# A one-core decoder layer: first layer norm in groups of tiles, one product for the last 64 shared channels

## The reference

```
x = x + attention(layernorm(x))            # 16 heads of 128, causal, W_Q W_K W_V W_O
x = x + cross_attention(layernorm(x), ctx) # 32 heads of 16, ctx 375 rows per sequence
x = x + moe(layernorm(x))

layernorm: (x - mean) / sqrt(var + 1e-5)
moe: shared expert: silu(x @ shared_gate.T) * (x @ shared_up.T) @ shared_down.T   # 704 channels
     routed: top 2 of 8 experts of 352 channels, weights normalised to sum 1
```

## Time and profile before

| what | value |
|---|---|
| median of three runs | 963.21 us |
| the profiled execution | 963.22 us |
| its span, first to last instruction | 961.4 us |
| TensorE busy | 928.0 us, 97% of the span |
| VectorE busy | 544.2 us, 57% |
| ScalarE busy | 455.5 us, 47% |
| GpSimd busy | 178.3 us, 19% |

### The profile page before, as it was taken

The page is one execution under the profiler, slowest core; times in us unless marked ns, Lnnn a source line. Parts: engine busy times, 40 slices in busy tenths (PEclk is TensorE's granted clock), DMA queues, the critical chain, the costliest instruction groups (busy, mean ns, idle before and its releaser), DMA issues.

```text
span 961.4 us, 17906 instructions
## 1 busy us (share of the span) xinstructions
PE 928.0 (97%) x7250; PEld 807.5 (84%) x7250; DVE 544.2 (57%) x1192; ACT 455.5 (47%) x1113; POOL 178.3 (19%) x137
## 2 busy tenths in 40 slices
PE   4999999999999999999999999999999999999995
PEld 3999999999999999877777777777778888999994
DVE  6254444444444445485645546555457766888882
ACT  3342323232323233446666666566575234665651
POOL 1220202020202022411011011011000710223232
PEclk9999999999999999999999999999999999999998
DMA  5210442020202003212110010010032685998973
GB/s 190 67 45 22 166 164 66 24 66 22 66 23 67 22 22 110 65 47 88 55 34 23 13 34 23 13 33 13 1 125 80 231 247 185 335 301 280 303 198 44
DMA packets 31329, 94.12 MB, mean 98 GB/s; under 512 B 6176, under 2 KB 9488, under 8 KB 29328
## 3 DMA queue, kind: packets, MB, share of 16 engines
q1 hardware_dynamic: 26944, 83.80, 25.6%
q0 software_dynamic: 4304, 9.19, 4.7%
HBM read 74.33 MB, written 16.81 MB: 95 GB/s over the span
## 4 chain that ended last, share of the span: by engine, by line
PE 90%; DVE 5%; ACT 2%; issue 1%; DMA 1%; SPq 0%; POOL 0%; DVEq 0%
PE bank L512 25%; PE bank L513 24%; PE bank L514 24%; PE bank L709 3%; PE bank L726 3%; PE bank L559 3%; PE bank L584 3%; PE bank L676 1%; PE bank L571 1%; PE bank L822 1%; PE bank L736 1%; PE bank L600 1%; PE bank L830 1%; DMA wqk_f<-wqk 1%; DVE kT L1528 1%
## 5 line engine op out<-in xcount | busy, mean ns | idle before, releaser
L1130 ACT ACTIVATE ee<-bank 125x448 f32<-125x448 f32 x192 | 91.0, 547 | 22.0 <-PE bank L709 21.0
L512 PE MATMUL bank<-xT_hi,wqk_hi 128*128 128x448 f32 x256 | 95.9, 375 | 1.4 <-DVE xT_lo L1367 1.4
L514 PE MATMUL bank<-xT_lo,wqk_hi 128*128 128x448 f32 x256 | 93.8, 366 | 0.0
L513 PE MATMUL bank<-xT_hi,wqk_lo 128*128 128x448 f32 x256 | 93.6, 365 | 0.0
L512 PE MATMUL bank<-wkv_hi,ctx_hi 128*125 128x512 f32 x192 | 80.3, 418 | 2.6 <-DVE kn L1519 2.0
L1367 DVE TENSOR_TENSOR E_lo<-F,E_hi 128x940 fp32r<-128x940 f32 (+2 forms) x62 | 81.0, 1330 | 2.4 <-ACT E_hi L966 2.3
L513 PE MATMUL bank<-wkv_hi,ctx_lo 128*125 128x512 f32 x192 | 76.1, 396 | 0.0
L514 PE MATMUL bank<-wkv_lo,ctx_hi 128*125 128x512 f32 x192 | 75.7, 394 | 0.0
L512 PE MATMUL bank<-wv_hi,xT_hi 128*112 128x256 f32 x256 | 72.2, 282 | 0.0
L513 PE MATMUL bank<-wv_hi,xT_lo 128*112 128x256 f32 x256 | 71.8, 280 | 0.0
L514 PE MATMUL bank<-wv_lo,xT_hi 128*112 128x256 f32 x256 | 71.7, 280 | 0.0
(11 more groups left out here) (323 smaller groups left out, 2401.0 us busy)
## 6 DMA issues: line engine op xcount, KB each, us to landing
F<-wexp SPq DMA_DIRECT2D x14, 1408.0 KB, 7.4
F<-wexp SPq DMA_DIRECT2D x14, 768.0 KB
wqk_f<-wqk SPq DMA_DIRECT2D x16, 512.0 KB, 3.4
ctx_f<-ctx SPq DMA_DIRECT2D x24, 250.0 KB, 2.7
slots<-zt SPq DMA_DIRECT2D x1, 5397.0 KB, 19.0
xg<-slots SPq DMA_DIRECT2D x21, 256.0 KB, 7.0
F<-moe SPq DMA_DIRECT2D x6, 768.0 KB, 6.8
wv_f<-wv SPq DMA_DIRECT2D x8, 512.0 KB, 3.6
```

The source lines that it names most:

```text
L512: e.matmul(out, a[0], b[0], start=first, stop=False)
L513: e.matmul(out, a[1], b[0], start=False, stop=False)
L514: return e.matmul(out, a[0], b[1], start=False, stop=last)
L1130: e.activation(ee[(4 * n + r) % 8][:, :], SX[r][0:MS, 0:4 * T], ACT.Exp, scale=0.25).then_inc(*x_exped.did((n, r)))
```

## The change

1. **First norm.** The seven tiles fall in three groups, `FIRST = ((0, 1), (1, 4), (4, NA))`. Root and refinement are done once for a group, on 1 or 3 columns (`first_root`, `first_scale`). The normed rows of tiles 0 to 4 are written by ScalarE as scale times x plus bias (`first_rows`), those of tiles 5 and 6 by VectorE; each tile has its own buffer and four banks instead of two take the turned tiles. The low part of the first query/key weights moves from GpSimd to VectorE. Its load moves ahead of the loads of tiles 4 to 6.
2. **Dummy transposes.** `warm(n)` issues n transposes of the identity into a bank that nobody reads: 14 before tile 0 is turned, 20 after it, 10 after tile 3.
3. **The last 64 channels.** Gate and up weights of block 5 now lie side by side in one 128-wide operand (gate in columns 0 to 63, up in 64 to 127), so that one group of 12 products gives both. `up_silu` reads partitions 0 to 63 and writes 64 to 127; `up_mul`, `up_hi`, `up_low` and the down product work on partitions 64 to 127. The block's weights are 1024 columns instead of 1536.
4. **The chain of that block, first half.** `up_low(0, 4)`, `up_mul(0, 5)` and the split of the down weights move to places between the small operations for `eid`.
5. **The first routed load's splits.** Part (3, 0) moves from unit 2 to the end of unit 1, part (3, 2) to the first place of unit 2. In unit 2 the hi part of the gathered rows comes ahead of `up_hi(1, 4)`, and `up_hi` and `up_low` of block 4 come behind part (3, 1).

```diff
+FIRST = ((0, 1), (1, 4), (4, NA))
...
             kind, j, k, second = its[n]
             if kind == "s":
-                return ([(1, 0), (1, 3)], [(2, 0), (2, 3)], {0: [(3, 0)], 2: [(3, 1), (3, 2)], 1: [(3, 3)]}.get(when))[k] if when == 2 or k == 2 else []
+                return {(0, 2): [(1, 0), (1, 3)], (1, 2): [(2, 0), (2, 3)], (1, 1): [(3, 0)], (2, 0): [(3, 2)], (2, 2): [(3, 1)],
+                        (2, 1): [(3, 3)]}.get((k, when), [])
...
             w.wait_ge(*id_in[0])
-            for j in range(NA + 2):
...
+            warm(14)
+            turn_first(0)
+            warm(20)
+            for i in range(1, 4):
+                turn_first(i)
+            warm(10)
+            qk_pe(0, 0, 0)
+            for i in range(4, NA):
+                turn_first(i)
+            qk_pe(0, 0, 1)
             qk_pe(0, 1, 0)
...
                 for k in range(KC):
-                    i = mm3(GU[u][:, 0:HT], at(p, ALL, toks(o + k * 256 + a * 128, 128)), at(xT, ALL, k, toks(n * HT, HT)),
-                            k == 0, k == KC - 1)
+                    z = o + (k * 128 if c == NS - 1 else k * 256 + a * 128)
+                    i = mm3(GU[u][:, 0:HT], at(p, ALL, toks(z, 128)), at(xT, ALL, k, toks(n * HT, HT)), k == 0, k == KC - 1)
...
                     if k:
                         up_pe(1, 2 * j + 1, 0)
-                    up_pe(1, 2 * j + 1, 1)
+                    if k < 2:
+                        up_pe(1, 2 * j + 1, 1)
...
             for c in (4, 5):
-                for a in range(2):
+                for a in range(2 if c == 4 else 1):
                     up_pe(0, c, a)
                 down_pe(c - 1)
...
+            first_stats(0)
+            first_scale(0)
+            for i in range(1, 4):
+                first_stats(i)
+            first_low(0)
+            first_scale(1)
+            first_stats(4)
+            w.wait_ge(*wqk_hi[0])
+            low(wqk[0][1][:, :, :], wqk_f[0][:, :, :], wqk[0][0][:, :, :]).then_inc(*wqk0_lo.did(0))
+            first_stats(5)
+            for i in range(1, 4):
+                first_low(i)
+            first_stats(6)
+            first_scale(2)
+            w.wait_ge(*scaled1[2])
+            for i in (5, 6):
+                e.tensor_scalar(xn_f[i][:, :], xa[:, i, :], mv[:, i, 0:1], rstd[:, i:i + 1], ALU.subtract, ALU.mult).then_inc(*xn_dve.did(i))
+            for i in range(4, NA):
+                first_low(i)
...
             up_low(0, 3)
             s_low(5, 0)
-            s_low(5, 1)
             rows_normal(2)
...
+            up_low(0, 4)
             do(e.tensor_tensor(le, le, le2, ALU.mult))
...
+            up_mul(0, 5)
+            s_low(5, 1)
             do(e.tensor_reduce(small["le2"][0:1, 0:NSL], le, X, ALU.add))
             e.tensor_scalar(eid[:, :], small["le2"][0:1, 0:NSL], float(NE - 1), None, ALU.min).then_inc(*eid_done.did(0))
-            up_low(0, 4)
-            s_low(5, 2)
-            up_mul(0, 5)
             up_low(0, 5)
...
+            wqk_load(0)
             for j in range(4, NA):
                 e.dma_start(xa[:, j, :], x_d[j]).then_inc(*x_in[j].did(0))
-            wqk_load(0)
```

More of the change, by code:

```diff
@@ L157, in decoder_layer @@
         place_z2 = place[0]
+        xn_f = [over(f"xn_f{i}", [128, D], F32, place_z + i * D * 4) for i in range(NA)]
+        assert place_z + NA * D * 4 <= place_z2
         nm = [sb(f"nm{i}", [T, 4], F32) for i in range(2)]
@@ L339, in piece @@
         def piece(k):
-            last = (3, WU, WU + SC)
+            last = (3, WU, WU + (LAST if k == 2 else SC))
             if jobs[k][0] == "s":
@@ L350, in decoder_layer @@
             prev = its[n - 1] if n else None
-            ups += [("b", j, a) for a in range(2)] if kind == "e" else [("u", 1, 2 * j + q, a) for q in range(2) for a in range(2)]
+            ups += [("b", j, a) for a in range(2)] if kind == "e" else [("u", 1, 2 * j + q, a) for q in range(2) for a in range(2) if 2 * j + q + a < NS]
             if prev and prev[0] == "e":
@@ L451, in decoder_layer @@
         gl_done, lg_done = sig("gl_done", range(NB)), sig("lg_done", range(NB))
-        third = [(c, p) for c in range(NS) for p in range(3)]
+        third = [(c, p) for c in range(NS) for p in range(3 if c < NS - 1 else 2)]
+        down_third = [2] * (NS - 1) + [1]
+        low_rows = slice(64, 128)
         s_hi, s_lo = sig("s_hi", third), sig("s_lo", third)
@@ L796, in down_pe @@
                 w.wait_ge(*h_lo[0, c])
-                w.wait_ge(*s_lo[c, 2])
+                w.wait_ge(*s_lo[c, down_third[c]])
+                part, z = (low_rows, D) if c == NS - 1 else (ALL, 1024)
                 for b in tiles:
@@ L1231, in up_hi @@
                 h_, to = (hh1, hs1) if n and j else (hh[j], hs[j])
-                hi(to[0][:, :], h_[:, :]).then_inc(*h_hi.did((n, c)))
+                part = low_rows if c == NS - 1 else ALL
+                hi(to[0][part, :], h_[part, :]).then_inc(*h_hi.did((n, c)))
             def part_hi(k, p):
@@ L1449, in o_add, with first_stats @@
                     e.tensor_tensor(xa[:, j, :], xa[:, j, :], PJ[u][:, :], ALU.add).then_inc(*pj_dve.did(u))
-            def aggregate(j):
-                e.bn_aggr(mv[:, j, :], st[:, j, :]).then_inc(*mv_done[1].did(j))
-            for j in range(NA + 2):
-                if j < NA:
-                    w.wait_ge(*x_in[j][0])
-                    e.bn_stats(st[:, j, :], xa[:, j, :]).then_inc(*own.step())
-                    ready = own.last()
-                if j == 0:
-                    w.wait_ge(*ready)
-                    aggregate(0)
-                if 1 <= j <= NA:
-                    i = j - 1
-                    def then():
-                        if j < NA:
-                            w.wait_ge(*ready)
-                            aggregate(j)
-                    if i > 1:
-                        w.wait_ge(*turned1[i - 2])
-                    norm_rows(1, i, 128, xa[:, i, :], xn[i % 2], then)
-                if j >= 2:
-                    norm_low(1, j - 2, 128, banks[6 + j % 2])
+            def first_stats(i):
+                w.wait_ge(*x_in[i][0])
+                stats(1, i, 128, xa[:, i, :])
@@ new lines, in first_scale @@
+            def first_scale(g):
+                a, b = FIRST[g]
+                y, tmp = rstd[:, a:b], rt[0][:, a:b]
+                w.wait_ge(*root_done[1][g])
+                e.scalar_tensor_tensor(tmp, y, -0.5, y, ALU.mult, ALU.mult).then_inc(*own.step())
+                w.wait_ge(*own.last())
+                e.scalar_tensor_tensor(tmp, mv[:, a:b, 1], LNE, tmp, ALU.add, ALU.mult).then_inc(*own.step())
+                w.wait_ge(*own.last())
+                e.scalar_tensor_tensor(y, tmp, 1.5, y, ALU.add, ALU.mult).then_inc(*own.step())
+                w.wait_ge(*own.last())
+                e.scalar_tensor_tensor(rt[1][:, a:b], mv[:, a:b, 0], -1.0, y, ALU.mult, ALU.mult).then_inc(*scaled1.did(g))
@@ L1630, in up_mul @@
             def up_mul(n, c):
-                g, h_ = ("u", n, c, 1), bufs(n, c)
+                g, h_ = ("u", n, c, 1 if c < NS - 1 else 0), bufs(n, c)
+                part = low_rows if c == NS - 1 else ALL
                 w.wait_ge(*gu_act["u", n, c])
@@ L1642, in up_low @@
                 w.wait_ge(*h_hi[n, c])
-                low(h_[2][1][:, :], h_[1][:, :], h_[2][0][:, :]).then_inc(*h_lo.did((n, c)))
+                part = low_rows if c == NS - 1 else ALL
+                low(h_[2][1][part, :], h_[1][part, :], h_[2][0][part, :]).then_inc(*h_lo.did((n, c)))
             def part_low(k, p):
@@ L2134, in part_load @@
                     o = WU if p == 3 else 0
-                    e.dma_start(F[k % 2][:, o:o + SC], moe_d[2 * j + (p == 3)]).then_inc(*to.did(k))
+                    z = LAST if k == 2 and p == 3 else SC
+                    e.dma_start(F[k % 2][:, o:o + z], moe_d[2 * j + (p == 3), :, 0:z]).then_inc(*to.did(k))
                 else:
```

128 lines of the change are left out of this document (81 added, 47 removed).

## The result

The changed kernel takes 956.25 us (median of 6 runs, 955.48 to 956.58) against 963.4 us of the kernel before in the same comparison (6 runs, 962.73 to 964.47): a ratio of 0.9924, 95% interval 0.9912 to 0.9937. The profiled execution took 956.54 us with a span of 954.8. The forecast was 954.3 and its range for 8 in 10 was 952.2 to 957.0. The time lies inside that range, but outside the forecast's own (up to 955.7).

A forecast was written before the change was run, and what follows sets the result against it. TensorE was taken as the bound, with 90% of the chain. Gains of 5.1 (start), 1.9 and 1.95 (block 5) sum to 8.95: 963.2 - 8.95 = 954.3 us; own range 952.3 to 955.7, for 8 in 10 952.2 to 957.0.

The forecast's parts named there:

- Start, 5.1 us: First stage: the first value product starts at 27.7 instead of 32.81 us, 5.1 us gained; lower bound 2.9.
- Rival A: Start: dummies don't raise TensorE's clock, so 2.9 us gained instead of 5.1; 956.5 us, chance 0.22.
- Block 5, first half, 1.9 us: Shared expert, first half of rows: twelve of 24 products go, 2.42 us, less a new wait; bounds 0.9 to 2.4.
- a new wait of 0.5 us: Block 5, first half: `up_low(0, 5)` ready at 756.3, while TensorE would want it at 755.8.
- Block 5, second half, 1.95 us: Shared expert, second half: twelve products go, 2.46 us, less longer waits around unit 2's down product; bounds 0.9 to 3.1.
- stream 512 columns each and save nothing: Block 5's down products on 64 partitions: they still stream 512 columns each, so no saving was counted.
- The moved splits: Job 3's splits, shared expert: cost nothing while part (3, 1) is ready for the first expert.
- The slack of 0.2 us: First expert: margin for part (3, 1), whose hi and low the twelve products cover; each 0.1 us late costs 0.1.
- Routed stage: Its loads move with TensorE and it keeps 6.7 us a unit, as long as TensorE stays busy.
- rival D: A later stage takes the start's gain back through a transfer not released by TensorE; 957.3 us, chance 0.05.
- Rival B: VectorE's chains in block 5 and at part (3, 1) run later, 3.85 falls to 1.5; 956.6 us, chance 0.09.
- Rival C: Clock stays at 1.2 GHz through the whole start, value products at 37.9; slower, 964.5 us, chance 0.01.

The follow-up runs named there:

- wv_late: The change, with GpSimd's first value-weight split held until VectorE has scaled the third group's statistics: 956.62 us, ratio 0.9938 to the kernel before.
- no_warm: The change without its 44 dummy transposes, else the same: 956.95 us, ratio 0.9935 to the kernel before.
- best2w_cold: The change without dummies, block 5's down products on 128 partitions, value split behind group 3's row passes, VectorE reordered: 954.14 us, ratio 0.9906 to the kernel before.
- down_full: The change, with block 5's two down products reading all 128 partitions, zeros in the weights' other half: 954.79 us, ratio 0.9915 to the kernel before.

## Why the prediction was near, and where it failed

- *Start, 5.1 us.* Right in mechanism and size: 32.81 to 27.48 is 5.3 (5.2 to 5.9 in the five traces with this start). The rise of the clock from dummies, the block of the small step beside GpSimd's split (1.07 us) and the first products at 15.0 instead of 15.5 were in the trace as laid out. Two things were not. ScalarE's new row pass took 0.81 us for one and 2.21 for three, where the sum had 0.6 and 1.7; that three rows were still done at 12.45 (forecast 12.4) is luck, since they began at 10.24 instead of 10.8. And the clock's rise, put at 8.3, came ahead of 7.4 in this trace, while in others with dummies it fell among the twenty (2.35 us for them here, 3.40 in `wv_late`). The weights' low part took 1.19, as taken.
- *Rival A, 956.5 us.* Refuted by the traces with dummies and by `no_warm`. That its number came out is chance: it put the loss at the start, and the loss is in block 5. The Trainium skill's rule from "TensorE: Matmul & The Clock Gate", Part 4: PE-mode transpose, which would have given this rival's time, does not hold for these transposes: before the rise ahead of 7.39 TensorE had done only 14 dummies and one tile's turn, in `best2w_cold` before the rise ahead of 15.55 only four tiles' turns, and in `no_warm` the products ran at 0.37 us.
- *Block 5, first half, 1.9 us.* Twelve products less gave the 2.42. The term that was too small is "a new wait of 0.5 us": the down product of block 4 and the wait behind it took 0.79 more than before. The 64-partition product with the group behind it took 0.32 more (0.21 and 0.11), which the sum had at zero. Of that 0.2 is the change back to full operands, gone in `down_full`, and 0.1 the slow step behind the new wait, which stayed there. What is left is 1.3.
- *Block 5, second half, 1.95 us.* 2.46 as said. The wait at unit 2's down product, with a first step of the expert that was 0.06 longer, cost 0.49 more than before, where I had 0.4 (0.7 in place of 0.3), so the chain of four steps on ScalarE and VectorE was sized well. The step that failed is "stream 512 columns each and save nothing": I gave the 64-partition products a cost of zero and no bounds, and they cost 1.08 us beyond the old ones, since they alternate with full ones. The wait at the third tile did not come, hidden behind the slow trios. What is left is 0.9.
- *The ranges.* The forecast's own range follows from 4 + 3.3 to 955.9, not 955.7; the measured 956.25 lies outside either. What went wrong is block 5 alone (1.3 + 0.9 = 2.2 against 3.85), which lies below even the 3.3 of that range. The wider range held because it had been stretched to take in A and B, neither of which came true.
- *The moved splits.* Put down as free. That is so, but it says too little: without them the removal of the products would have given back 1.45 us. The slack of 0.2 us held: no wait for `E_lo` stands in the trace of the change.
- *Routed stage.* Untouched, as said: rival D is out. Rival B (VectorE's chains later) had the right size, 956.6, by another cause; its VectorE chains were later by 0.3 and 0.1 us only. Rival C, slower than before, never was near; its terms as written (3.7, 9.5, 28 x 0.217, 48 x 0.373) add up to 37.2, not to its 37.9.

Sum by the traces: 5.3 + 1.3 + 0.9 = 7.5, less the 0.3 us by which the stretch between start and block 5 was longer in this execution, 7.2; forecast 8.95. The 0.6 us behind the last product, which the profiled execution lost, are not in the medians' 7.15.

## What to carry to other kernels

Where part of an operand is dropped, look at how its pieces alternate on TensorE: here fewer partitions saved no time, and each change of the range cost some 0.18 us, so leaving the zeros in was faster. When half of a group of products goes, the other engines' steps that it covered become the path; move them first. Two engines that block each other are not parted by moving one past the nearest operation that it holds up, but past all that it holds up.

## What the runs showed of the hardware that I had not expected

- A change of the partitions that TensorE's operands occupy (all 128, or 64 to 127) cost 0.09 us ahead of it and 0.09 us behind it, every time, and the weight load didn't start ahead of its product there. A stop for another engine has the same step of 0.32 us behind it (807.42 to 807.74 in the trace before), so the 0.18 looks like a short stop, made without anybody being waited for; what makes it isn't shown. Products of 96 partitions (from 0 on) among full ones showed no such step: 0.24 us ahead of one (811.21 to 811.45). Whether it is the number of partitions or where they begin wasn't tried.
- Transposes, 14 of an identity and four of a tile, were all that TensorE had done when its clock rose to the 2.4 GHz level ahead of 7.39 us, and it was still there at the first product, 15.00 us, after waits of 1.35 and 0.74 us.
- A VectorE row pass took 0.54 us alone and 2.70 us beside GpSimd's split, to just behind the split's end; three low parts that read a bank took 1.89 in both cases. GpSimd's split of the value weights took 2.35 to 2.40 us whatever ran beside it.
